# Second layer: maximum scores of two heads side by side in halves of the array, in a burst at each slot's end

## The reference

```python
x = x + _L0_attn_ref(_layernorm(x), ...)   # causal, 16 heads of 8
x = x + _L0_ffn_ref(_layernorm(x), ...)    # 8 experts, 2 per row
x = x + _L1_attn_ref(_layernorm(x), ...)   # 16 heads of 8, no mask
x = x + _L1_ffn_ref(_layernorm(x), ...)    # gate, up, down in 4-bit blocks
# L1 attention
scores = jnp.einsum('bhtd,bhsd->bhts', q, k) / jnp.sqrt(HD)
probs = jax.nn.softmax(scores, axis=-1)
attn = jnp.einsum('bhts,bhsd->bhtd', probs, v)
# L1 feed-forward
h = jax.nn.silu(fp4_linear(x, w_gate)) * fp4_linear(x, w_up)
return fp4_linear(h, w_down)
```

## Time and profile before

| | us |
|---|---|
| median of 3 runs | 2320.85 |
| profiled execution | 2317.76 |
| its span | 2316.0 |
| PE busy, share of the span | 2038.6, 88% |
| DVE busy | 1621.9, 70% |
| ACT busy | 1390.4, 60% |
| first stack issue of layer one (L1319) | at 1185.3 |
| first max score of layer one | at 1194.7 |
| first exp score of layer one | at 1219.5 |

### The profile page before, as it was taken

How to read it: one execution, slowest core, us unless ns; L and a number is a source line. 1 busy time by engine, 2 the same in 40 slices (tenths; PEclk the granted TensorE clock), 3 DMA queues, 4 the chain that set the end, 5 groups by cost and what they waited for, 6 DMA issues and landing times.

```text
span 2316.0 us, 45088 instructions
## 1 busy us (share of the span) xinstructions
PE 2038.6 (88%) x13603; PEld 1060.0 (46%) x13603; DVE 1621.9 (70%) x4772; ACT 1390.4 (60%) x3097; POOL 1063.4 (46%) x1777
## 2 busy tenths in 40 slices
PE   2999999999999939999649999999999999999984
PEld 1455455554554429999613333333333333333333
DVE  3888888887888633321137888888888888888854
ACT  0466666666666624444207777777777776777772
POOL 6433746537455250000265656555565655654222
PEclk8899999999999969999859999999999999999997
DMA  5232223223222024444322222121222212121100
GB/s 175 81 93 67 85 74 91 73 71 92 71 89 82 20 73 143 144 142 140 90 73 66 73 58 68 54 62 54 66 59 57 70 55 60 55 64 50 47 6 14
DMA packets 154335, 174.12 MB, mean 75 GB/s; under 512 B 38448, under 2 KB 122096, under 8 KB 153968
## 3 DMA queue, kind: packets, MB, share of 16 engines
q1 hardware_dynamic: 144464, 153.85, 22.6%
q0 software_dynamic: 8192, 16.79, 2.5%
q10 hardware_dynamic: 1440, 0.60, 0.1%
HBM read 120.30 MB, written 49.28 MB: 73 GB/s over the span
## 4 chain that ended last, share of the span: by engine, by line
PE 27%; DVE 12%; issue 5%; ACT 4%; POOL 2%; DMA 0%; SPq 0%; ACTq 0%; DVEq 0%; POOLq 0%
PE bank L1560 8%; PE bank L1538 6%; DVE l_rowmax L1770 6%; PE bank L1548 6%; ACT l_probs L1679 3%; DVE l_h L1790 1%; PE bank L1593 1%; PE bank L1574 1%; DVE l_hq L199 1%; PE bank L1631 1%; DVE l_hq L216 1%; DVE l_stats L1804 1%; DVE l_hq L222 1%; PE bank L1621 1%; PE bank L1579 1%
## 5 line engine op out<-in xcount | busy, mean ns | idle before, releaser
L1770 DVE TENSOR_REDUCE l_rowmax<-bank 128x1 f32<-128x512 f32 x1024 | 642.7, 682 | 109.6 <-PE bank L1538 109.4
L1679 ACT ACTIVATE l_probs<-bank 128x512 f32<-128x512 f32 x1024 | 549.1, 605 | 134.8 <-PE bank L1548 134.5
L865 DVE CUSTOM_DVE_ANT_0 bank<-bank,mask_rows_q 128x512 f32<-128x512 f32 (+3 forms) x1024 | 476.6, 518 | 101.9 <-PE bank L625 95.6
L781 ACT ACTIVATE l_probs<-bank 128x512 f32<-128x512 f32 (+3 forms) x1024 | 389.2, 443 | 150.0 <-PE bank L637 144.0
L1538 PE MATMUL bank<-k_stack,q_stack 96*128 96x512 bf16 x1024 | 395.0, 387 | 68.9 <-DVE l_rowmax L1770 43.9
L1548 PE MATMUL bank<-q_stack,k_stack 128*128 128x512 bf16 x1024 | 387.3, 382 | 1.6 <-ACT l_probs L1679 1.4
L625 PE MATMUL bank<-k_stack,q_stack 96*128 96x512 bf16 (+3 forms) x1024 | 316.8, 314 | 25.4 <-DVE l_rowmax L865 14.8
L635 PE MATMUL bank<-q_stack,k_stack 128*128 128x512 bf16 (+3 forms) x1024 | 307.6, 308 | 0.2
L1560 PE MATMUL bank<-l_probs,v_aug 128*32 128x512 f32 x2048 | 272.8, 605 | 29.4 <-ACT l_probs L1679 28.7
L637 PE MATMUL bank<-mask_rows_k,ident_bf 128*128 128x128 bf16 x1024 | 221.1, 221 | 0.0
L1174 ACT ACTIVATE experts_hT<-bank,experts_b 128x256 f32<-128x256 f32 x288 | 118.3, 471 | 158.2 <-PE bank L1136 158.2
(11 more groups left out here) (259 smaller groups left out, 3015.7 us busy)
## 6 DMA issues: line engine op xcount, KB each, us to landing
q_stack<-scratch SPq DMA_DIRECT2D x384, 96.0 KB
k_stack<-scratch SPq DMA_DIRECT2D x384, 96.0 KB
experts_w<-in_w SPq DMA_DIRECT2D x72, 256.0 KB, 2.4
scratch<-l_q_parts SPq DMA_DIRECT2D x32, 384.0 KB, 2.7
scratch<-l_k_parts SPq DMA_DIRECT2D x32, 384.0 KB, 3.0
experts_rows<-rows_in SPq DMA_DIRECT2D x72, 128.0 KB, 2.1
rows_out<-experts_y SPq DMA_DIRECT2D x72, 128.0 KB, 2.1
q_stack<-l_rowmaxT SPq DMA_DIRECT2D x384, 4.0 KB
```

Of the source, the lines that this page charges most:

```text
L781: nc.scalar.activation(probs[:, (a * HG + j) % PSLOTS, c0:S], bank[:, c0:S], ACT.Exp, scale=SCALE).then_inc(t_read, 1)
L865: nc.vector.tensor_tensor_reduce(scores, scores, m["mask_rows_q"][:, S - keys(t):S], 1.0, LOWEST, ALU.add, ALU.max, rowmax[:, g % 2, c:c + ...
L1679: nc.scalar.activation(probs[:, (a * HG + j) % PSLOTS, :], bank[:, :], ACT.Exp, scale=SCALE).then_inc(t_read, 1)
L1770: nc.vector.tensor_reduce(rowmax[:, g % 2, c:c + 1], bank[:, :], X_AXIS, ALU.max).then_inc(s_read, 1)
```

## The change

Before, the scores for the maximum used 96 rows of the array for one head. After, the stack is laid out so that 64 rows (8 of the 9 products of parts) lie in one half of the array: for heads 0 and 1 of a group in rows 0 to 63 (the ninth product in rows 64 to 71, the maxima in rows 96 to 98, as before), for heads 2 and 3 in rows 64 to 127 (the ninth product in rows 0 to 7, the maxima in rows 32 to 34). `scores_for_max` issues two matmuls of 64 rows, of heads j and j + 2, which go to the two banks of one **pair**, and DVE takes both heads' maxima in one instruction over 1024 numbers. Ring s is two pairs (four banks), ring t has three banks instead of four. Both pairs stand at the slot's end, after END and `probs_v`, which has moved there too. `out` moves from MIDDLE to the head of END, up takes two tiles at a time, `take_out` moves from the fourth exponential to before the second one of the slot after. AHEAD is 10, and the maxima's way shifts by a slot. The stack comes in 14 DMAs for a group instead of 6, the maxima in 6 instead of 3. The rows of heads 2 and 3 that stay constant are written by DVE in the experts stage, six memsets over 2048 numbers per partition in four tiles' time. Everything before layer one is the same but for these memsets.

```diff
+S_PAIRS = 2
+T_BANKS_1 = 3
-AHEAD = 9
+AHEAD = 10
+def stack_parts(sp, stacks, scratch, g, stacked):
+    for which, stack in enumerate(stacks):
+        for half in range(2):
+            slots = g * HG + 2 * half
+            base = which * PARTS * P * S + slots * S
+            def copy(row, part, step, blocks):
+                sp.dma_start(stack[row:row + blocks * D, slots:slots + 2, :].rearrange("p h t -> p (h t)"),
+                             bass.AP(scratch.tensor, base + part * P * S, [[step * P * S, blocks], [H * S, D], [1, 2 * S]])
+                             ).then_inc(stacked, 16)
+            for i in range(PARTS):
+                blocks = PARTS if half == 0 or i < PARTS - 1 else PARTS - 1
+                if which == 0:
+                    copy(HALF * half + SLAB * i, i, 0, blocks)
+                else:
+                    copy(HALF * half + SLAB * i, 0, 1, blocks)
+            if half:
+                copy(0, PARTS - 1, 0, 1)
...
-    MIDDLE = [("rowmax", g, 4 * g + 5) for g in range(G)] + [("out", g, F + 4 * g + 8) for g in range(G)] + [
+    MIDDLE = [("rowmax", g, 4 * g + 6) for g in range(G)] + [
         ("xnT", 0, -15), ("xqT", 0, F + 32)] + [("turn", k, F + 44) for k in range(NC)]
-    END = [("v", 0, 0), ("qk", 0, -9), ("qk", 1, -8)]
...
+    END = [("out", g, F + 4 * g + 6) for g in range(G)] + [("v", 0, 0), ("qk", 0, -9), ("qk", 1, -8)] + [("gate", t, F + 33) for t in range(2)] + [("up", 0, F + 33)] + [
+        ("gate", t, F + 33) for t in range(2, TT)] + [("up", 1, F + 33), ("down", 0, F + 45), ("down", 1, F + 53)]
...
-    POOL_WORK = [("split_max", g, 4 * g + 4) for g in range(G)]
+    POOL_WORK = [("split_max", g, 4 * g + 5) for g in range(G)]
...
-    SP_WORK = [("max_out", g, 4 * g + 6) for g in range(G)] + [("parts", 0, -6), ("parts", 1, -5)]
+    SP_WORK = [("max_out", g, 4 * g + 7) for g in range(G)] + [("parts", 0, -6), ("parts", 1, -5)]
...
-            def scores_for_max(a, j):
+            def scores_for_max(a, pair):
...
+                banks = s_pair(("max", a, pair))
                 t = TT - 1 - t
-                nc.tensor.matmul(bank[:, :], q_stack[b % 2][0:MAXROW, h_, t * P:(t + 1) * P],
-                                 k_stack[b % 2][0:MAXROW, h_, :], start=True, stop=True).then_inc(s_mm, 1)
+                for half in range(2):
+                    rows, h_ = slice(HALF * half, HALF * (half + 1)), g * HG + pair + 2 * half
+                    last = nc.tensor.matmul(banks[:, half * S:(half + 1) * S], q_stack[b % 2][rows, h_, t * P:(t + 1) * P],
+                                            k_stack[b % 2][rows, h_, :], start=True, stop=True)
+                last.then_inc(s_mm, 1)
...
                     if j == HG // 2:
-                        if uses.exp_quad(s - 1) is not None:
-                            probs_v(uses.exp_quad(s - 1))
                         for kind, b, k in due(MIDDLE, s):
...
-                    if a is not None:
-                        scores_for_max(a, j)
                 for kind, b, k in due(END, s):
+                    if kind == "out":
+                        turned_out(b, k)
...
+                if uses.exp_quad(s - 1) is not None:
+                    probs_v(uses.exp_quad(s - 1))
+                if a is not None:
+                    for pair in range(2):
+                        scores_for_max(a, pair)
...
-                    if j == HG - 1 and uses.exp_quad(s - 1) is not None and uses.exp_quad(s - 1) % TT == TT - 1:
-                        take_out(*divmod(uses.exp_quad(s - 1) // TT, G))
+                    if j == 1 and uses.exp_quad(s - 2) is not None and uses.exp_quad(s - 2) % TT == TT - 1:
+                        take_out(*divmod(uses.exp_quad(s - 2) // TT, G))
...
-                nc.vector.tensor_reduce(rowmax[:, g % 2, c:c + 1], bank[:, :], X_AXIS, ALU.max).then_inc(s_read, 1)
+                largest = rowmax[:, g % 2, :].rearrange("p (k i t) -> p i k t", k=2, t=TT)[:, pair, :, TT - 1 - t]
+                nc.vector.tensor_reduce(largest, banks[:, :].rearrange("p (k n) -> p k n", k=2), X_AXIS, ALU.max).then_inc(s_read, 1)
```

More of the change, by code:

```diff
@@ L255, with __init__ @@
 T_BANKS = 4
-AHEAD = 9
+S_PAIRS = 2
+T_BANKS_1 = 3
+AHEAD = 10
 class Uses:
-    def __init__(self, NB, middle, end, ring_of, first, last, ahead, only):
+    def __init__(self, NB, middle, end, ring_of, first, last, ahead, only, pairs):
         self.NB, self.ahead, self.only = NB, ahead, only
@@ L281, in __init__ @@
                 use(ring_of[key[0]], key)
+            if self.max_quad(s) is not None and pairs:
+                for pair in range(2):
+                    use("s", ("max", self.max_quad(s), pair))
     def max_quad(self, s):
@@ L1821, in _ @@
                         read(kind, b, k)
+                if uses.max_quad(s) is not None:
+                    for pair in range(2):
+                        take_max(uses.max_quad(s), pair)
                 for kind, b, k in due(DVE_WORK, s):
```

132 lines of the change are left out of this document (68 added, 64 removed).

## The result

The changed kernel took 2429.9 us (median of 4 runs, 2424.3 to 2436.8), beside 2319.6 for the kernel before in the same comparison (2317.4 to 2321.3). The ratio is 1.048, with a 95% interval of 1.045 to 1.051: 110 us slower. The forecast was 2335, with a range up to 2392, so the direction was right, the size was not, and the time lies outside the range.

A forecast was written before the change was run, and what follows sets the result against it. PE was taken to bound layer one, a batch going from 67.4 to 67.9 us. +6, +5, +2 and +1 made +14 on 2317.8, so 2332, and 3 for the median: 2335; range 2270 to 2392.

The forecast's parts named there:

- Together 2.0, from 0.5 to 5: Layer one: PE's waits for pairs that DVE reads late, 2.0 us a batch, from 0.5 to 5.
- rival 5: Layer one: the burst starves DVE, long pieces hit harder, waits of 5 instead of 2; +40, 2375 us; chance 7%.
- What goes from PE: Bare slot: two half matmuls side by side cost one; slot 2.50 us before ring waits, 5.6 less a batch.
- Ring t with three banks: Each slot's fourth exp score waits for the first's read: 0.43 us a bare slot, 11.0 a batch with other pieces' waits.
- Take-out's share: In three slots the first END piece waits for a read behind take-out, 0.59 us long: 1.29 each, 3.9 a batch.
- DVE's instruction: DVE in layer one: two heads' maxima at once take 1.13 us; a slot's maxima fall from 2.40 to 2.26.
- Batches 0 and 1: Start of layer one, no feed-forward part: both together go from 105.4 to 110.5 us, +5.
- rival 4: SP is late: third group's maxima come after their scores' turn, 2 to 4 us a batch; 2360 to 2390; chance 8%.
- The 7.6 for a group's stack: SP's DMA issues for one group's stack take 7.6 us instead of 3.5.
- The rest: Outside the batches: front +2 us, end +1, memsets in the experts stage hidden, 0 taken.
- Rival 2: Layer one: waits for ring t and pairs overlap, together below 12.5 us a batch; faster, 2251 us; chance 33%.
- the forecast's own 14: Whole kernel: +6 for 13 batches, +5 for batches 0 and 1, +2 front, +1 end, in us.

The follow-up runs named there:

- experiments 1 and 2: Changed kernel with ACT's rounding of h's quotient (hsizes) one slot later: 2371.2 us; then ACT's normalising of x (normalise4) one slot later too: 2358.3 us.
- experiment 5: Kernel of experiment 2 with take-out ahead of the slot's first exponential instead of between first and second: ratio 1.005 to the kernel before, on another chip.
- experiment 4: Kernel of experiment 2 with the first pair of maximum scores in the slot's middle, before the third exp score: 2343.0 us, ratio 1.012 to the kernel before.
- experiment 2: Changed kernel with ACT's hsizes and normalise4 each one slot later: 2358.3 us, ratio 1.020 to the kernel before.

## Why the prediction was wrong, point by point

- **The step that failed** is DVE's part, "Together 2.0, from 0.5 to 5". It asked only whether PE must wait for a pair, and that came out at 1.1 a batch. DVE's pieces have other readers: ACT rounds the quotient of h, POOL works on the statistics of x and ACT on its result. I moved the maxima to the slot's end, put the scores for exp next to each other, and left what this does to these readers at nothing. It took a spare time of 1.8 us from the first handoff and put a wait of 3.3 in its place, more by ACT's coming earlier (3.4 us) than by DVE's coming later (1.7). The two handoffs cost 59 and 13 us (experiments 1 and 2, by medians; by the ratios 54 and 11). The sum had no term for them, and rival 5, which names DVE's long pieces, priced them at 40 by waits for pairs, so it had the right neighbourhood and the wrong reader.
- **The clock** was in no term. The wait of 3.1 us was followed by 6 us at about half the granted clock, 2.2 us more in each of twelve batches, 26 of the 59.
- **What goes from PE:** right. Halves side by side (0.60 for four; 1.03 where they share rows), bare slot 2.94 for 2.93, the step from the halves to the next score 0.32 for 0.31 (0.54 for it and one plain step).
- The page "TensorEngine Tiling (Array Packing)" of the Trainium skill, section Key Properties, says that a change of mode drains the engine. The trace agrees as far as that the third change has a price: the step from the halves to the next score has some 0.10 more than a plain one. A drain itself is not seen.
- **Ring t with three banks:** right. The fourth score came 1.08 after the first, as worked out. With the handoffs away a batch was 68.9, where the forecast, which did not have them, is 67.9. Take-out's share was real too: 20 us of waits ahead of the first END pieces went with it in experiment 5.
- **DVE's instruction:** right. 1.217 us shown, two in 2.36, so a step of 1.14 for 1.13.
- **Batches 0 and 1:** +12 for +5. The price of a slot was right; rival 4, SP late, is true in these two alone, where slots are short: 3.5 us for the third group's maxima in batch 0 and 1.4 in batch 1. In full batches there is no such wait. The 7.6 for a group's stack does not follow from its terms, as six issues at 0.75 and eight at 0.41 are 7.8; 7.5 was measured, and nothing hangs on the difference.
- **The rest:** the front -1 for +2, the end +4 for +1, the memsets hidden as said.
- **Rival 2** (waits overlap, 2251) had a third of the chance and got nothing: 13 us of waits a batch were counted and about 14 came, the two handoffs left out (68.9 less 54.9 of PE's own work). In experiment 4 waits did overlap, but the other way: taking one away let the next show.

Added up: 59 + 13 for the handoffs and 7 too little for batches 0 and 1 make 79; with the forecast's own 14 that is 93. The other 17 are about 13 for a batch of 68.9 instead of 67.9, and 4 for the one batch in which PE waited for POOL and its late gather (experiment 2). That gather's idle time is in one profiled execution, and its cause stays open.

## What to carry to other kernels

When a change moves one engine's work within a period, list every reader of what that engine makes, on all engines, and what stands behind each reader in its queue; here the reader that the change is about was not the one that stalled. A handoff that had no idle time in the trace of before may have had little to spare, here 1.8 us: work it out from the end of the one piece and the start of the other, and move both sides, since a reader that now gets there earlier takes as much from it as a writer that gets there later. And an idle gap on PE costs more than its length if the clock falls behind it: here gaps of 3.1 us cost 5.3 each.
